# DLRM tower on one core: first ids by a DMA of ACT's queue, a tenth table for all tiles, layer 1's dense parts at other places and one PSUM bank per tile

## The reference

```python
e = jnp.stack([tbl_0[ids[:, 0]], ..., tbl_25[ids[:, 25]]], axis=1)        # 512 x 26 x 128
combined = jnp.concatenate([e, r_dense_x[:, None, :]], axis=1)            # 27 vectors per sample
interact = jnp.einsum('bfd,bgd->bfg', combined, combined)
z = interact[:, TRIU_I, TRIU_J]                                           # 351 pairs
h = jnp.concatenate([z, r_dense_x], axis=1)                               # 479
h = jnp.maximum(h @ W_top1 + b_top1, 0.0)                                 # 479 x 512
h = jnp.maximum(h @ W_top2 + b_top2, 0.0)                                 # 512 x 256
y = h @ W_top3                                                            # 256 x 1
```

## Time and profile before

| | |
|---|---|
| median of 3 runs | 104.04 us (104.0 to 105.1) |
| the profiled execution's own time | 103.44 us |
| its span, first to last instruction | 101.6 us |
| busy in the span | PE 92.5, DVE 61.0, ACT 59.7, POOL 61.6 us |
| granted TensorE clock | 1.00 throughout |

### The profile page before, as it was taken

One profiled execution on the slowest core, in us unless ns is written; L12 is line 12 of the kernel. 1 busy time (PEld: TensorE's weight loads), 2 busy tenths in 40 slices (PEclk: granted clock), 3 DMA queues, 4 the chain that ended last, 5 costly groups with the idle time before them and its releaser, 6 DMA issues.

```text
span 101.6 us, 3386 instructions
## 1 busy us (share of the span) xinstructions
PE 92.5 (91%) x1452; PEld 75.7 (74%) x1452; DVE 61.0 (60%) x97; ACT 59.7 (59%) x113; POOL 61.6 (61%) x69
## 2 busy tenths in 40 slices
PE   3979798999999999999999889998899989999990
PEld 3948474868877676868887889788787869968870
DVE  2499799999999999999694320046200470036201
ACT  5099999999999999999942014005440045403040
POOL 3777777777777777787777777777777730000000
DMA  1669999997889758899922221221122210000000
GB/s 48 210 230 242 230 233 224 224 240 223 176 245 254 246 158 209 195 236 351 346 65 58 52 58 52 58 58 52 52 58 58 52 52 6 0 6 6 0 0 1
DMA packets 6716, 13.37 MB, mean 132 GB/s; under 512 B 2031, under 2 KB 3311, under 8 KB 6702
## 3 DMA queue, kind: packets, MB, share of 16 engines
q1 hardware_dynamic: 4718, 9.10, 33.2%
q0 software_dynamic: 1984, 4.07, 15.6%
HBM read 13.16 MB, written 0.00 MB: 129 GB/s over the span
## 4 chain that ended last, share of the span: by engine, by line
PE 48%; DVE 27%; issue 11%; ACT 7%; DMA 3%; SPq 1%; DVEq 0%; ACTq 0%
DVE onehot L568 16%; PE ps_gram L321 13%; PE ps_h L357 11%; DVE table_lo L557 8%; PE ps_h L298 6%; PE ps_h L379 6%; DMA table_raw<-in_tbl 3%; PE ps_h L352 3%; ACT away L463 3%; PE ps_tp L308 3%; PE ps_gram L298 3%; PE ps_tp L379 2%; ACT table_hi L454 2%; DVE zT L601 1%; DVE gramT L585 1%
## 5 line engine op out<-in xcount | busy, mean ns | idle before, releaser
L263 POOL DMA_INDIRECT rows<-in_tbl,ids_sb x62 | 60.8, 981 | 20.0 <-issue 18.6
L568 DVE TENSOR_TENSOR onehot<-ids_bc,ps_h 125x1536 fp32r<-125x1536 int16 (+2 forms) x20 | 32.2, 1610 | 0.0
L298 PE MATMUL ps_gram<-onehot,table_hi 125*128 125x512 f32 x72 | 28.9, 414 | 2.0 <-DVE onehot L568 1.6
L298 PE MATMUL ps_gram<-onehot,table_lo 125*128 125x512 f32 x72 | 27.4, 397 | 0.2 <-DVE table_lo L557 0.2
L490 ACT COPY featT<-ps_tp 128x512 f32<-128x512 f32 (+3 forms) x18 | 10.2, 588 | 15.7 <-PE ps_tp L308 15.6
L298 PEld LDWEIGHTS ps_gram<-onehot,table_hi 125*128 125x128 f32 x72 | 13.4, 188 | 8.0 <-DVE onehot L568 4.6
L298 PEld LDWEIGHTS ps_gram<-onehot,table_lo 125*128 125x128 f32 x72 | 13.5, 188 | 3.6 <-DVE table_lo L557 0.8
L557 DVE TENSOR_TENSOR table_lo<-table_raw,table_hi 125x512 fp32r<-125x512 f32 x22 | 15.0, 687 | 1.5 <-ACT table_hi L454 1.5
L463 ACT ACTIVATE away<-ids_bc,vnr 125x512 f32<-125x512 int16 (+1 forms) x22 | 14.3, 718 | 0.0
L321 PE MATMUL ps_gram<-featT 128*26 128x26 f32 x1024 | 13.2, 193 | 0.9 <-issue 0.3
L321 PEld LDWEIGHTS ps_gram<-featT 128*26 128x26 f32 x1024 | 11.0, 107 | 4.0 <-issue 3.3
(11 more groups left out here) (50 smaller groups left out, 65.9 us busy)
## 6 DMA issues: line engine op xcount, KB each, us to landing
table_raw<-in_tbl SPq DMA_DIRECT2D x11, 448.0 KB
w<-in_W SPq DMA_DIRECT2D x6, 256.0 KB
ids_bc<-in_ids_lookup SPq DMA_DIRECT2D x10, 128.0 KB, 5.7
rows<-in_tbl,ids_sb POOLq DMA_INDIRECT x62, 4.0
table_raw<-in_tbl SPq DMA_DIRECT2D x11, 52.0 KB
denseT<-in_denseT SPq DMA_DIRECT2D x1, 256.0 KB, 4.2
b2w<-in_b2w SPq DMA_DIRECT2D x1, 256.0 KB
ids_sb<-in_ids SPq DMA_DIRECT2D x1, 52.0 KB, 1.8
```

The lines of the kernel that those rows point to most:

```text
L263: nc.gpsimd.indirect_dma_start(out=rows[:, t % ROWB, n, :], out_offset=None, in_=tables[f], in_offset=bass.IndirectOffsetOnAxis(ap=ids_sb[ ...
L298: last = nc.tensor.matmul(table_bank[k][:, at:B], (table_hi, table_lo)[part][:, k % 2, c, :], onehot[:, k % 2, c, at:B], start=n == 0, sto ...
L568: nc.vector.tensor_tensor(onehot[:, k % 2, c:end, at:B], ids_of(k, 0).rearrange("k (o b) -> k o b", o=1).broadcast_to(part), row.rearrange ...
```

## The change

- **First ids.** ids_bc[:, 0] comes by a DMA that ACT issues before anything else. PE's broadcast and DVE's cast of the ids are gone; PE's warm-up is 12 matmuls in one piece instead of 4 + 4 with the broadcast between. ACT works on table 0's ids (write_away, write_onehot) ahead of its split_hi(0), no longer behind it.
- **FULL = 10.** Table 9 is looked up for all 512 samples; tile 0 has 16 gathers (61 in all). gram(0, 0) waits for table 9's copy, and lookup(10) now stands between gram(0, 0) and gram(0, 1).
- **Dense parts and their loads.** The dense matmuls of tile 0 stand behind lookup(6), those of tile 1 behind gram(0, 1), of tile 2 behind gram(1, 1), and those of tile 3 half behind gram(2, 1), half behind gram(3, 1). SP loads denseT behind table 4 and the dense rows of W1 behind table 5; before, they came behind table 7 and table 10.
- **A bank per tile.** Tiles 0 to 2 use ps_h1[t % 2] for all 512 columns; the matmuls are ordered by input chunk, and ReLU starts when a tile's layer 1 is complete. Transposes of gathered groups stand at other places.

```diff
-FULL = 9
+FULL = 10
-WARM = 8
+WARM = 12
-GROUPS = [[4, 4, 4, 3, 2], [4, 4, 4, 3], [4, 4, 4, 3], [4, 4, 4, 2, 1]]
+GROUPS = [[4, 4, 4, 4], [4, 4, 4, 3], [4, 4, 4, 3], [4, 4, 4, 2, 1]]
-GROUPS_AFTER = {2: [0], 3: [1], 4: [2], 5: [3], 6: [4], 7: [5], 8: [6, 7]}
+GROUPS_AFTER = {2: [0], 3: [1], 4: [2], 5: [3], 7: [4], 8: [5], 9: [6]}
+DENSE_AFTER = 6
...
-        vnr_ps = ps_h1[1][0:VK, 0, 0:VC]
+        vnr_ps = ps_z[0:VK, BANK // P - 1, 0:VC]
...
+        def h1_of(t, n):
+
+            if t < TILES - 1:
+                return ps_h1[t % 2][:, n, :]
+            return ps_h1[1 - n // (C1 // 2)][:, n % (C1 // 2), :]
...
-                if k == FULL - 2:
+                if k == RAW + 1:
                     sp.dma_start(denseT[:, :, :], denseT_in.rearrange("d (t p) -> d t p", p=P)).then_inc(dense_in, 16)
-            for c in range(ZC + 1):
+                if k == RAW + 2:
+                    sp.dma_start(w1[:, ZC, :], W1[:, ZC, :]).then_inc(w1_dense_in, 16)
+            for c in range(ZC):
                 load_w1(c)
...
-            keep_busy(WARM // 2)
-            broadcast_first_ids()
-            keep_busy(WARM // 2)
+            keep_busy(WARM)
             pe.wait_ge(ident_ready, 1)
             for k in range(FULL):
                 lookup(k)
                 for n in GROUPS_AFTER.get(k, []):
                     transpose_group(n)
+                if k == DENSE_AFTER:
+                    layer1_dense(0)
             gram(0, 0)
             lookup(FULL)
             gram(0, 1)
             transpose_group(FIRST[2] - 1)
-            lookup(FULL + 1)
+            layer1_dense(1)
+            transpose_group(FIRST[2])
             transpose_z(0)
-            dense(0)
+            transpose_group(FIRST[2] + 1)
             pairs(0)
             gram(1, 0)
             layer2(0)
             gram(1, 1)
-            dense(1)
-            for n in range(FIRST[2], FIRST[3] - 1):
-                transpose_group(n)
+            layer1_dense(2)
+            transpose_group(FIRST[2] + 2)
             transpose_z(1)
-            transpose_group(FIRST[3] - 1)
+            transpose_group(FIRST[2] + 3)
             pairs(1)
...
-            dense(2)
+            layer1_dense(TILES - 1, range(C1 // 2))
             transpose_group(FIRST[3])
             transpose_group(FIRST[3] + 1)
             transpose_z(2)
-            transpose_group(FIRST[3] + 2)
             pe.wait_ge(zT_done, TILES - 1)
             for c in range(ZC):
-                layer1_pairs(2, 0, c)
-            transpose_group(FIRST[3] + 3)
-            for c in range(ZC - 1):
-                layer1_pairs(2, 1, c)
-            transpose_group(FIRST[3] + 4)
-            layer1_pairs(2, 1, ZC - 1)
+                layer1_pairs(2, c)
+                transpose_group(FIRST[3] + 2 + c)
             t = TILES - 1
             gram(t, 0)
             layer2(t - 1)
             gram(t, 1)
-            dense(t)
+            layer1_dense(t, range(C1 // 2, C1))
...
+            act.dma_start(ids_bc[:, 0, :], spread(0)).then_inc(bc_in[0], 16)
             act.wait_ge(vnr_copied, 1)
             nc.scalar.activation(away[:, 0, 0, 0:VC], vnr[0:VK, :], ACT.Abs).then_inc(warm_done, 1)
             act.wait_ge(warm_done, 1)
-            split_hi(0)
             write_away(0)
             write_onehot(0)
+            split_hi(0)
```

More of the change, by code:

```diff
@@ L188, in packed, with ids_of, spread @@
             return z[:, t % 2, GAT[g]:GAT[g + 1]].rearrange("p (j i) -> p j i", i=GPITCH[g])
[L190 to L197, removed]
+        def ids_of(k):
+            return ids_bc[0:VK, k, first_tile(k) * P:B]
+        def h1_of(t, n):
+            if t < TILES - 1:
+                return ps_h1[t % 2][:, n, :]
+            return ps_h1[1 - n // (C1 // 2)][:, n % (C1 // 2), :]
+        def spread(k):
+            return ids_lookup[:, k * B:(k + 1) * B].broadcast_to([P, B])
         block = ctx.enter_context(nc.Block())
@@ L272, in keep_busy @@
                 for _ in range(count):
-                    nc.tensor.matmul(ps_z[:, 0:ZC, :], ident_r[:, :],
+                    nc.tensor.matmul(ps_h1[0][:, 0:ZC, :], ident_r[:, :],
                                      ident_r[:, :].rearrange("k (o p) -> k o p", o=1).broadcast_to([P, ZC, P]),
                                      start=True, stop=True)
[L277 to L283, removed]
             def lookup(k):
@@ L341, in transpose_last_z, with layer1_dense @@
                 nc.tensor.transpose(last_z[c][0:ZK], z[:, t % 2, c * ZK:(c + 1) * ZK], ident[:, :]).then_inc(ztp_last, 1)
-            def layer1_dense(t, half):
+            def layer1_dense(t, columns=range(C1)):
                 if t == 0:
[L346 to L358, removed]
+                    pe.wait_ge(dense_in, 16)
+                    pe.wait_ge(w1_dense_in, 16)
+                elif 2 <= t < TILES - 1 or columns[-1] < C1 // 2:
+                    pe.wait_ge(h1_relu, C1 * (t - 1))
+                elif t == TILES - 1:
+                    pe.wait_ge(h1_relu, C1 * t)
@@ new lines, in layer1_dense, with layer1_pairs @@
+                for n in columns:
+                    nc.tensor.matmul(h1_of(t, n), w1[:, ZC, n * P:(n + 1) * P], denseT[:, t, :],
+                                     start=n == 0 or t == TILES - 1 and n == C1 // 2, stop=False)
+            def layer1_pairs(t, c, columns=range(C1)):
+                for n in columns:
+                    last = nc.tensor.matmul(h1_of(t, n), w1[0:ZK, c, n * P:(n + 1) * P], zT[0:ZK, c, t % 2, :],
+                                            start=False, stop=c == ZC - 1 and n == columns[-1])
@@ L359, in layer1_pairs @@
                 if c == ZC - 1:
                     last.then_inc(h1_done, 1)
-            def dense(t):
-                layer1_dense(t, 0)
-                layer1_dense(t, 1)
             def pairs(t):
+                if t == 0:
+                    pe.wait_ge(w1_in, 16 * ZC)
                 pe.wait_ge(zT_done, t + 1)
-                for half in range(2):
-                    for c in range(ZC):
-                        layer1_pairs(t, half, c)
+                for c in range(ZC):
+                    layer1_pairs(t, c)
@@ L444, in _ @@
                 for half in range(2):
-                    layer1_pairs(t, half, c)
+                    layer1_pairs(t, c, range(half * C1 // 2, (half + 1) * C1 // 2))
             layer2(t)
@@ L462, in write_away @@
                     c = VC - ACHUNKS[k] + a
-                    nc.scalar.activation(away[:, k % 2, a, at:B], ids_of(k, 1), ACT.Abs,
+                    nc.scalar.activation(away[:, k % 2, a, at:B], ids_of(k), ACT.Abs,
                                          scale=-1.0, bias=vnr[0:VK, c:c + 1]).then_inc(away_done, 1)
@@ L566, in write_onehot @@
                 part = [VK, end - c, B - at]
-                row = vnr[0:VK, c:end] if k == 0 else vnr_ps[:, c:end]
                 nc.vector.tensor_tensor(
                     onehot[:, k % 2, c:end, at:B],
-                    ids_of(k, 0).rearrange("k (o b) -> k o b", o=1).broadcast_to(part),
-                    row.rearrange("k (c o) -> k c o", o=1).broadcast_to(part),
+                    ids_of(k).rearrange("k (o b) -> k o b", o=1).broadcast_to(part),
+                    vnr_ps[:, c:end].rearrange("k (c o) -> k c o", o=1).broadcast_to(part),
                     ALU.is_equal).then_inc(onehot_dve, 1)
```

74 lines of the change are left out of this document (31 added, 43 removed).

## The result

The change takes **108.07 us** (median of four runs, 107.66 to 108.2) beside 104.02 (103.69 to 105.1) for the kernel before on the same chip: 1.0398 times, 95% interval 1.0348 to 1.0448. The forecast was +2.0 us, the measurement is +4.05, above the range. The profiled execution took 108.02 us, span 106.2, against 103.44 and 101.6: 4.6 of span, of which 0.6 is how far the profiled execution of before lies under its median.

A forecast was written before the change was run, and what follows sets the result against it. DVE was taken to bound the table phase, PE's stops in its hand-written order the end. End +3.4 less start 1.4 gave +2.0 us: 105.4 on the profiled execution, 106.0 on the median, range 104.2 to 107.6.

The forecast's parts named there:

- The start: From launch to DVE's split of table 1: the new ids DMA lets the table phase begin 1.4 us earlier.
- L: Landing time of table 0's ids by ACT's DMA, taken as 3.4 us, between 2.5 and 6.4.
- Table 1's split: DVE's split of table 1 moves from 11.20 to 9.67 us, or near 9.8 with table 1's later landing.
- Carrying through: Table phase: the start's 1.4 us shift persists because DVE has no gap in it.
- Early loads and dense(0): Table phase: denseT and W1 loads ahead of tables 5 and 6, tile 0's dense matmuls behind lookup(6), costed at nothing.
- The end, +3.4: From table 9 on: the longer lookup and new order of PE's work delay the end by 3.4 us.
- pairs(0): Tile 0's pair matmuls start at 62.56 instead of 59.85 on before's clock, +2.71 us.
- from gram(1, 1)'s end to pairs(1): Tile 1's chain through DVE and z's transposes takes 3.69 us, where before it took 3.93.
- pairs(1) to pairs(2): The stretch from 71.90 to 84.06 stays unchanged, because DVE limits its last part.
- pairs(2) to gram(3, 0): Tile 2's pairs get 0.96 us longer: four added transposes, and four matmuls no longer covering the last group's copy.
- the start gains nothing: Rival, chance 0.15: ids land at 4.9 or later, or table 5 or 6 comes late; 107.6 us.
- PE's work decides: Rival, chance 0.13: behind table 9 PE's work, not its stops, sets the time; only the start's gain remains, 102.6 us.

The follow-up runs named there:

- e4: Changed kernel, ACT's ids DMA reading 128 different 1 KB pieces instead of one piece 128 times; disturbed chip, no valid time; first one-hot at 3.96 us.
- e9: Changed kernel with table 0's ids broadcast by a DMA on SP's queue right behind ids_sb instead of on ACT's; 107.87 us, 1.0381.
- e8b: Kernel before with dense(0) behind lookup(6), early loads, a PSUM bank per tile, tile 3's last groups a step earlier; 104.25 us, 1.0014.
- e1c: Changed kernel with the old start (PE's broadcast of table 0's ids, no ACT DMA for them); four runs, 107.55 to 109.57 us.
- e11: e1c with the warm-up as 24 matmuls of 128 columns instead of 8 of 384, 32 PE instructions more; 1.0323, median 106.9 us.
- e6: Changed kernel with tile 3's last groups transposed one step earlier; disturbed chip, no valid time; pairs(2) to gram(3, 0) 3.21 us instead of 4.08.
- e10: e8b with the warm-up as 24 matmuls of 128 columns instead of 8 of 384, 32 PE instructions more; 1.024 times the kernel before.
- e7b: Changed kernel with old start, gram(0, 1) ahead of lookup(10), tile 2's groups behind gram(1, 1), tile 3's last groups a step earlier; 107.39 us, 1.0327.

## Why the prediction was wrong

- **The start is the step that failed.** Its sum was L + 6.2, with a landing L taken at 3.4 between 2.5 and 6.4; L was 5.2 (4.5 us after the issue), 1.8 more. I chose by nearness to ids_sb, which brings each partition its own piece; the rows of ids_bc, which I set aside as queued behind a table, read their source just as the new DMA does, and their lowest, 4.2, was the near one. e4 gives 1.3 us of the 1.8 to the one-piece source; the other 0.5 is open. e9 shows that the queue isn't it.
- **Table 1's split** came at 11.46, not at 9.67 or 9.8, and a term was missing: PE, idle behind its warm-up, did table 0 at half clock and held DVE for 0.37. Together the start lost 0.70 instead of gaining 1.4: 2.1 of the 2.6 us by which the span's +4.6 exceeds the forecast of +2.0. The other 0.5 is the end's. (Between the medians the error is 2.1, 108.07 for 106.0: the prediction added 0.6 to get from before's profiled execution to the median, and the change's profiled execution, 108.02, lies at its median.)
- By the Trainium skill's fit for one DMA of POOL's path ("DMA: Bandwidth & Descriptors", "Anatomy of one DMA") the estimate was 2.3 us from issue to landing; the traces of these two, issued by ACT, have 4.5 for the one-piece source, and 3.2 for the spread one.
- **Carrying through** table 9 was right: +0.70 at table 2, +0.69 at table 9. Early loads and dense(0) cost nothing seen (e8b). That the start costs 0.7 us of the whole time isn't shown by a run: e1c's fastest, 107.55 beside 108.07, fits it, e1c's others don't, and e11 can't tell, as its own start is 0.5 late.
- **The end, +3.4, was right in its parts.** From the last one-hot of table 9, 0.69 late: gram(0, 0) expected at 52.99, came at 52.97; pairs(0) expected +2.71, got +3.83 less 0.69, so +3.14, the extra being the block's end at 56.49 (0.83 us from one matmul to the next, where 0.17 is usual); from gram(1, 1)'s end to pairs(1) 3.70 (72.24 to 75.94) for 3.69, though the work between the two pairs took 0.44 more, unexplained (63.68 to 72.24, 8.56 for 8.12); pairs(1) to pairs(2) 0.45 less (11.71 for 12.16); pairs(2) to gram(3, 0) +0.88 for 0.96. In all 3.9 for 3.4. That the errors of the parts nearly cancel is luck in part; only the last term is shown alone, by e6.
- **The rival "the start gains nothing", 107.6,** was the nearest: right on the landing (4.9 or later), and only 0.5 short, as it left no room for a loss. "PE's work decides" is out: PE stood ahead of z in tiles 0 and 1 (0.29, 0.85) and in tile 2 (0.56).
- **Not seen by any rival:** PE's supply of instructions. In the change it is some 0.5 us at 56.49; in e10 it decided, and in the profiled runs of e1c and e7b. Why one kernel's runs differ by 2 us and more (e1c 107.55 to 109.57, e8b 103.66 to 107.16), and whether the faster ones have the stops at all, is open.

## What to carry to other kernels

Price a DMA by the row that reads its source the same way, not by the one with the same place in a queue. Where an engine runs hundreds of tiny instructions, count its instructions: the end of a block of 256 behind such a run was a stop of up to 1.9 us here, and an edit ahead of it, be it 16 matmuls of warm-up, moves it. So a time that doesn't follow from the work should be read for "issue" first, and an ordering judged with the block's end shifted as well.

## What the runs showed of the hardware

- Instructions come in packets of 16 KB (11 of them); PE stopped at instruction 685 or 941 of its own count, or at both, 256 apart, in before, the change, e1c, e7b, e8b, e9 and e10, for 0.3 to 1.9 us. The block behind a gram was there 3.3 (e9) to 4.1 us (e10) after that gram's start, while PE needs 1.8 us for the gram.
- Stops of 1.6 to 1.9 us behind a gram were followed by PE at half clock in e1c (0.50 from 57 to 60), e7b, e8b and e10, those of 0.3 and 0.5 in before and the change were not. In e10, 15 matmuls of lookup(9) then took 4.2 us, where 16 took 3.0 before, so the 1.9 us stop cost over 3.
- A DMA of 128 KB that reads one 1 KB piece for all partitions took 4.5 us on ACT's queue and 4.3 on SP's; with a different piece for each partition 3.2 (e4).
- A 52 KB DMA on SP's queue took 4.0 us to land instead of 1.8 when ACT issued the broadcast at the same time, and the gather that waits for it began at 5.02 instead of 2.79.
- 24 matmuls of 128 columns kept PE busy longer than 8 of 384: with the broadcast between, PE ended at 8.6 us (e11) instead of 6.1 (before), as a matmul of 128 columns took 0.22 us.
